# Two-layer transformer block on one core: the opening stages and the store of the rotated halves, arranged anew

## The reference

```python
q = (x @ Wq.T).reshape(B, S, H, hd).transpose(0, 2, 1, 3)   # k and v likewise
q, k = _rope(q), _rope(k)        # [t1*cos - t2*sin, t1*sin + t2*cos], t1, t2: halves of a head
scores = jnp.einsum('bhqd,bhkd->bhqk', q, k) * scale
```

## Time and profile before

| | |
|---|---|
| median of 3 runs | 652.36 us (646.97 to 653.94) |
| the profiled execution | 647.78 us, its span 646.1 us |
| PE busy | 549.5 us (85%) |
| DVE busy | 396.2 us (61%) |
| ACT busy | 309.1 us (48%) |
| POOL busy | 212.8 us (33%) |

### The profile page before, as it was taken

One profiled execution on the slowest core, in us unless ns is written; L12 is line 12 of the kernel. 1 busy time (PEld: TensorE's weight loads), 2 busy tenths in 40 slices (PEclk: granted clock), 3 DMA queues, 4 the chain that ended last, 5 costly groups with the idle time before them and its releaser, 6 DMA issues.

```text
span 646.1 us, 10027 instructions
## 1 busy us (share of the span) xinstructions
PE 549.5 (85%) x3586; PEld 308.5 (48%) x3586; DVE 396.2 (61%) x932; ACT 309.1 (48%) x589; POOL 212.8 (33%) x276
## 2 busy tenths in 40 slices
PE   2877989787879897799878998999999999899873
PEld 1833435434435454444435555545575446643632
DVE  6368887576767555565765576756656765434463
ACT  2223756575455752466435555554435432564221
POOL 4544543242633731650352311414331110220101
PEclk9576999999899898899989999999999999999998
DMA  8461214211343462201561122125404120000000
GB/s 225 107 171 42 77 38 97 68 53 58 136 113 62 98 156 90 100 35 59 107 166 65 57 51 47 41 80 128 89 14 91 27 51 1 19 2 0 1 17 16
DMA packets 28545, 46.15 MB, mean 71 GB/s; under 512 B 5104, under 2 KB 14352, under 8 KB 27920
## 3 DMA queue, kind: packets, MB, share of 16 engines
q1 hardware_dynamic: 28496, 45.52, 27.4%
HBM read 27.22 MB, written 17.83 MB: 70 GB/s over the span
## 4 chain that ended last, share of the span: by engine, by line
PE 57%; DVE 20%; ACT 6%; issue 5%; SPq 5%; DMA 3%; POOL 3%; POOLq 0%; DVEq 0%; ACTq 0%
PE ps L565 11%; PE ps L522 9%; PE ps L628 8%; DVE NM L1124 6%; PE ps L493 5%; PE ps L490 4%; PE ps L495 4%; PE ps L516 2%; DVE terms L1224 2%; PE ps L650 2%; PE ps L748 2%; DVE stats L1108 2%; PE ps L674 2%; PE ps L572 1%; PE ps L611 1%
## 5 line engine op out<-in xcount | busy, mean ns | idle before, releaser
L1124 DVE TENSOR_REDUCE NM<-ps 128x1 f32<-128x512 f32 (+3 forms) x352 | 219.5, 639 | 120.0 <-PE ps L495 113.0
L785 ACT ACTIVATE PG<-ps 128x512 f32<-128x512 f32 x320 | 181.4, 596 | 160.9 <-PE ps L522 93.6
L522 PE MATMUL ps<-QS,K 128*128 128x512 f32 x320 | 118.6, 455 | 0.6 <-DMA QS<-MP 0.6
L495 PE MATMUL ps<-maskb,identb 128*128 128x128 bf16 x512 | 111.1, 235 | 0.0
L565 PE MATMUL ps<-PG,V 128*32 128x512 f32 (+3 forms) x1024 | 98.4, 458 | 6.7 <-POOL PG L1070 5.2
L493 PE MATMUL ps<-K,QS 96*128 96x256 f32 (+3 forms) x256 | 84.8, 375 | 15.4 <-DVE NM L1124 15.1
L490 PE MATMUL ps<-KS,QS 96*128 96x256 bf16 (+3 forms) x256 | 74.7, 327 | 20.5 <-DVE NM L1124 19.3
L495 PEld LDWEIGHTS ps<-maskb,identb 128*128 128x128 bf16 x512 | 52.4, 102 | 38.7 <-issue 31.4
L522 PEld LDWEIGHTS ps<-QS,K 128*128 128x128 f32 x320 | 51.6, 195 | 39.6 <-issue 21.1
L516 PE MATMUL ps<-QS,KS 128*128 128x128 bf16 (+3 forms) x256 | 63.8, 311 | 6.3 <-DMA QS<-scr 4.2
L1029 POOL TENSOR_TENSOR whole<-terms 128x512 f32<-128x512 f32 x28 | 35.4, 1273 | 101.4 <-DVE terms L1224 65.1
(11 more groups left out here) (153 smaller groups left out, 658.6 us busy)
## 6 DMA issues: line engine op xcount, KB each, us to landing
scr<-QC SPq DMA_DIRECT2D x24, 512.0 KB, 3.1
QS<-scr SPq DMA_DIRECT2D x64, 128.0 KB
QS<-scr_q SPq DMA_DIRECT2D x16, 288.0 KB
KS<-scr_k SPq DMA_DIRECT2D x16, 288.0 KB
QS<-scr SPq DMA_DIRECT2D x64, 64.0 KB
scr_k<-room SPq DMA_DIRECT2D x40, 64.0 KB, 2.1
scr_q<-room SPq DMA_DIRECT2D x24, 64.0 KB, 2.1
x<-in_x SPq DMA_DIRECT2D x4, 256.0 KB, 5.8
```

Of the source, the lines that this page charges most:

```text
L495: return pe.matmul(dst[:, P * (k - 1):P * k], identb[:], maskb[:, 0, :], start=False, stop=True)
L522: mm = pe.matmul(bank.rearrange("p (h q) -> p h q", h=HG), keys[:, SEQ[n] % 2, P * j:P * j + P], QS2[:, heads, P * i:P * i + P], start=(ke ...
L785: act.activation(PG[:, n % 2, unit_place(LAYER[n], (u + k) % UNITS), :], ps[:, ST0 + (u + k) % 3, :], ACT.Exp, scale=scale).then_inc(exp_d ...
L1124: dve.tensor_reduce(dst, src, AX.X, ALU.max, negate=True).then_inc(fill_read, 1)
```

## The change

- The scratch of layer 1 becomes one tensor with both halves of a part side by side. `halves` is [part, half, token] in place of `up` and `vp`. The outputs of the projection are ordered anew, so that U holds channels 0 to 3 of q and of k, and V channels 4 to 7. store1 is 5 DMAs of 256 KB from 128 partitions. load1 reads the same 72 rows from the new layout.
- The projection's weights are loaded plain (one DMA of 512-byte pieces, with v's) and put in order by two DVE copies into `wuv_sb`. The rotation table is loaded in 8 DMAs of 16 rows. QKV_LOADS has 9 DMAs.
- The weight product takes four heads at once: weights with 128 rows, `wkvb_sb` with four blocks on a diagonal of zeros, 64 columns: 8 matmuls. DVE clears `wkvb_sb` before all else. The operands come in 12 DMAs of 32 partitions from ACT's queue, at the head of its program, behind a wait for the clear. LOADS keeps 12.
- Of batch 0, DVE makes the V half's join and its two subtractions, and ln1n in place of ACT.
- One semaphore for each half or buffer replaces the shared ones.

```diff
-        QKV_LOADS = ((wqkv_sb[:, 0:2, 0:64], wqkv[:, 0].rearrange("c (a m) -> c a m", a=2)),
-                     (wqkv_sb[:, 0, 64:P], wqkv[:, 2, 64:P]), (wqkv_sb[:, 1, 64:P], wqkv[:, 2, 0:64]),
-                     (wqkv_sb[:, 2], wqkv[:, 4]), (rope1_sb[:], rope1[:]))
-        LOADS = ((wqn_sb, wq_nope[:]), (wo2_sb, wo2[:]), (wkvb_sb, wkvb[:]), (erow_sb, expert_rows[:]),
+        QKV_LOADS = [(wqkv_sb[:], wqkv[:, 0:5:2])]
+        QKV_LOADS += [(rope1_sb[2 * H * d + H * s:2 * H * d + H * s + H], rope1[H * d:H * d + H]) for d in range(D1 // 2) for s in range(2)]
+        LOADS = ((erow_sb, expert_rows[:]),
...
+        BLOCK_LOADS = []
+        for h in range(HG):
+            rows, heads = slice(NOPE * h, NOPE * h + NOPE), slice(G * h, G * h + G)
+            BLOCK_LOADS += [(wqn_sb[rows], wq_nope[:, heads]), (wo2_sb[rows], wo2[:, heads]), (wkvb_sb[rows, :, h, :], wkvb[:, heads])]
...
-                    sp.wait_ge(ready, 2 * (b + 1))
-                    sp.dma_start(scr_q[b, a, 0:64], up[0:64, a, :]).then_inc(stored1, 16)
-                    sp.dma_start(scr_q[b, a, 64:P], vp[0:64, a, :]).then_inc(stored1, 16)
+                    for k in range(2):
+                        sp.wait_ge(ready[k], b + 1)
                     for copy in ((a, 3 + a) if a < 2 else (a,)):
-                        sp.dma_start(scr_k[b, copy, 0:64], vp[64:P, a, :]).then_inc(stored1, 16)
-                        sp.dma_start(scr_k[b, copy, 64:P], up[64:P, a, :]).then_inc(stored1, 16)
+                        sp.dma_start(scr_1[b, copy].rearrange("k p t -> p k t"), halves[:, a]).then_inc(stored1, 16)
...
-                    for h in range(H):
-                        mm = pe.matmul(dst[:, LAT * h:LAT * h + LAT], w[:, h, :], wkvb_sb[:, h, :], start=True, stop=True)
+                    for g in range(G):
+                        mm = pe.matmul(dst[:, 0:H * LAT].rearrange("c (h g r) -> c g h r", h=HG, g=G)[:, g], w[:, g, :],
+                                       wkvb_sb[:, g], start=True, stop=True)
...
+            act.wait_ge(blocks_zero, 1)
+            for dst, src in BLOCK_LOADS:
+                act.dma_start(dst, src).then_inc(loaded, 16)
...
+                dve.wait_ge(loaded_qkv, ALL_QKV)
+                for k in range(2):
+                    dve.tensor_copy(wuv_sb[:, k, :].rearrange("c (d s h) -> c d s h", d=D1 // 2, s=2),
+                                    wqkv_sb[:, 0:2, P // 2 * k:P // 2 * k + P // 2].rearrange("c s (d h) -> c d s h", h=H))                       .then_inc(wuv_ready, 1)
                 dve.wait_ge(consts_ready, STACK_ZEROS)
...
+                if b == 0:
+                    dve.tensor_tensor(whole[:, j % 2, :], terms[:, j % 2, 0, :], terms[:, j % 2, 1, :], ALU.subtract)\
+                       .then_inc(whole_ready[j % 2], 1)
+
+            def parts1(b, _):
+                if b == 0:
+                    j = JOB0["k1", 0, 0] % 2
+                    dve.wait_ge(high1[1], 1)
+                    dve.tensor_tensor(terms[:, j, 0, :], whole[:, j, :], halves[:, 0, 1, :], ALU.subtract).then_inc(rest1[1], 1)
...
+            def ln1n(b, _):
+                if b == 0:
+                    dve.wait_ge(scale_ready, SCALE_OF["ln1n", 0])
+                    for t in range(NT):
+                        last = dve.tensor_scalar(xn[:, t, :], xs[0][:, t, :], rstd[0][:, t:t + 1], nmean[0][:, t:t + 1],
+                                                 ALU.mult, ALU.add)
+                    last.then_inc(xn_ready, 1)
...
+            dve.memset(wkvb_sb.rearrange("p g h r -> p (g h r)"), 0.0).then_inc(blocks_zero, 1)
             dve.memset(KS1[64:P].bitcast(F32), 0.0).then_inc(consts_ready, 1)
```

More of the change, by code:

```diff
@@ L304, in block_program @@
         room1 = sb("room1", [P, 4 * T])
[L305 to L306 removed]
+        halves = room1[:, 0:3 * T].bitcast(BF16).rearrange("p (a k t) -> p a k t", a=3, k=2)
         xT1 = room1[:, 3 * T:4 * T]
@@ L436, in load1 @@
                 heads = slice(HG * g, HG * g + HG)
[L437 to L440, removed]
+                first = 10 * b * P + HG * g
+                rows = [[2 * H * T, 3 * D1], [0, 3], [1, HG * T]]
+                sp.dma_start(QS1[0:72, heads, :], bass.AP(scr_1, first * T, rows)).then_inc(stack1_in[g], 16)
+                rows = [[2 * H * T, 3 * D1], [2 * P * T, 3], [1, HG * T]]
+                sp.dma_start(KS1[0:72, heads, :], bass.AP(scr_1, (first + H) * T, rows)).then_inc(stack1_in[g], 16)
             def store2(stage):
@@ L819, in parts1 @@
             def parts1(b, _):
-                for k, (stage, parts) in enumerate((("q1", up), ("k1", vp))):
+                for k, stage in enumerate(("q1", "k1")):
                     j = JOB0[stage, b, 0]
-                    act.wait_ge(whole_ready, j + 1)
+                    act.wait_ge(*joined(j))
                     if b and k == 0:
                         act.wait_ge(stored1, STORED1 * b)
-                    act.activation(parts[:, 0, :], whole[:, j % 2, :], ACT.Copy).then_inc(high1, 1)
+                    act.activation(halves[:, 0, k, :], whole[:, j % 2, :], ACT.Copy).then_inc(high1[k], 1)
             def parts1b(b, _):
-                for k, (stage, parts) in enumerate((("q1", up), ("k1", vp))):
+                for k, stage in enumerate(("q1", "k1")):
                     j = JOB0[stage, b, 0]
-                    act.wait_ge(rest1, 2 * b + k + 1)
-                    act.activation(parts[:, 1, :], terms[:, j % 2, 0, :], ACT.Copy).then_inc(middle1, 1)
+                    act.wait_ge(rest1[k], b + 1)
+                    act.activation(halves[:, 1, k, :], terms[:, j % 2, 0, :], ACT.Copy).then_inc(middle1[k], 1)
             def v1(b, _):
@@ L1027, in _ @@
                     j = JOB0[stage, b, part]
+                    if stage == "k1" and b == 0:
+                        return
                     pool.wait_ge(terms_ready, j + 1)
                     pool.tensor_tensor(whole[:, j % 2, :], terms[:, j % 2, 0, :], terms[:, j % 2, 1, :], ops[part % 2])\
[L1030 removed]
+                        .then_inc(whole_ready[j % 2], 1)
                 return _
             def parts1(b, _):
[L1034 removed]
+                for k, stage in enumerate(("q1", "k1")):
                     j = JOB0[stage, b, 0] % 2
[L1036 to L1037 removed]
+                    if b == 0 and k == 1:
+                        break
+                    pool.wait_ge(high1[k], b + 1)
+                    pool.tensor_tensor(terms[:, j, 0, :], whole[:, j, :], halves[:, 0, k, :], ALU.subtract).then_inc(rest1[k], 1)
             def parts1b(b, _):
[L1040 removed]
+                for k, stage in enumerate(("q1", "k1")):
                     j = JOB0[stage, b, 0] % 2
[L1042 to L1044 removed]
+                    if b == 0 and k == 1:
+                        break
+                    pool.wait_ge(middle1[k], b + 1)
+                    pool.tensor_tensor(halves[:, 2, k, :], terms[:, j, 0, :], halves[:, 1, k, :], ALU.subtract).then_inc(low1[k], 1)
+                    pool.wait_ge(low1[k], b + 1)
                     pool.sem_inc(job_done[j], 1)
```

52 lines of the change are left out of this document (30 added, 22 removed).

## The result

| | before | after |
|---|---|---|
| median | 653.15 us (4 runs, 646.97 to 655.77) | 643.50 us (4 runs, 640.79 to 645.14) |
| profiled execution | 647.78 us, span 646.1 | 640.79 us, span 638.8 |

The ratio of after to before is 0.9866, 95% interval 0.9821 to 0.9910: 1.3% faster. A second measurement gave 0.9868 (0.9825 to 0.9911), with medians of 653.52 (23 runs of before) and 643.72 (6 runs of after).

A forecast was written before the change was run, and what follows sets the result against it. Two almost equally long queues, PE's weight product and SP's sixteen stores, were taken to bound the first score. Terms -6.5 - 1.6 - 0.6 = -8.7 us gave 639.1 profiled, 643.7 on the median; range 636 to 651.

The forecast's parts named there:

- Opening: Start of the kernel up to the first score: batch 1's projection and first score 6.5 us earlier, score near 32.0.
- the step on the loads: SP's nine opening loads: last issued near 6.1, landed 9.5 to 10.5; cost 0 to 1.4 us through DVE's clear.
- a rival (646.5 with 2 to 3 us lost): Opening loads land late, at 12 to 13, and batch 0 loses 2 to 3 of the 6.5 us: 646.5, chance 0.20.
- DVE and POOL side by side: Batch 0's V half on DVE beside U on POOL: the engines exclude each other, 0.5 us more, V ends at 21.7.
- Norm on DVE: Batch 0's norm: four DVE operations in 0.87 us where ACT's took 1.66, -0.8 us.
- Twelve issues on ACT: Twelve opening loads on ACT's queue: 0.45 us each, done near 8, no cost; up to +1 if issues are dear.
- DVE's first clear: Memset of 128x256 ahead of everything on DVE: +0.22 us on the chain.
- The bytes are the same: Opening loads on a second queue: same bytes and 16 engines, so no bandwidth gain, zero in the sum.
- Weight product: Batch 0's product on PE at L650: 2.3 to 3.4 us instead of 13.36, off the path to batch 1's projection.
- Slower: Rival: without the long weight product PE's clock rises later and the gain is lost: 659, chance 0.10.
- Group 0's load: Load before the first scores: 4.9 us to land, in by 31.3 at the latest, slack 0.7 us.
- Later stalls: PE's waits behind SP's stores at batch 2 (-1.6) and batch 3 (-0.6) vanish.

The follow-up runs named there:

- the table early: Changed kernel with the rotation table loaded in one DMA, rows put in order by the host: first score 32.06 us, total 640.54 us.
- POOL's clear: Changed kernel with the clear of the rows from 96 given to POOL instead of DVE: first score 34.46 us.
- product only: Kernel before with eight block matmuls, their clear and twelve loads on ACT's queue, sixteen stores kept: ratio 1.0000, first score 37.85 us.
- sixteen stores for all: Changed kernel with every batch's store, batch 0's too, cut into 16 DMAs: total 652.22 us, first score 38.33 us.
- statistics first: Changed kernel with one-load table, projection awaiting weights alone, rows from 96 cleared by POOL, batch 1's statistics before V's low part: ratio 0.9820, median 640.21 us.
- the store alone: Kernel before with only the new layout, copies, nine opening loads and five stores a batch: ratio 0.9936, first score 40.81 us.

## Why the prediction came out

The total was forecast as 643.7 and is 643.5; the gain on the medians 8.7 forecast, 9.7 measured, between the two profiled executions 7.0. The mechanism is the forecast one: PE's queue and SP's both shortened, and the first score earlier only with both. That the total agrees to 0.2 us is luck: two terms of the sum were mis-sized, in opposite directions, and the median of before, 652.36 in three runs, is 653.15 with the fourth.

- *Opening, -6.5 forecast, -4.9 measured.* Mis-sized was the step on the loads. The last piece of the table was put at 9.5 to 10.5, no cost up to 10.6. It was issued at 6.08, as forecast, and landed 5.44 us later, at 11.52. And behind the copies stood 0.91 us of issue before the clear, which the forecast had not counted. In the chain of waits of after:

```profile
6.08 5.44 DMA rope_sb<-in_rope
...
11.91 0.91 issue
12.82 1.30 DVE KS L1226
```

  The clear ended at 16.29, not at 13.7 to 14.5. The prediction gave this as a rival (646.5 with 2 to 3 us lost); it came true, with 1.6 us lost. With the table early the first score is at 32.06, where the forecast had 32.0.
- *DVE and POOL side by side.* The two operations lose 0.9 us (1.06 + 1.20 instead of 2 x 0.69), where the forecast allowed 0.5. From the rotation's end to V's low part it is 4.5 us (18.80 to 23.29), where the forecast had 4.6 (17.1 to 21.7): the stage is right, the 1.6 us stand ahead of it. The Trainium skill, SBUF — State Buffer, "Who interferes with whom", says that such a pair, a VectorE operation with two SBUF inputs and a GpSimd one that reads SBUF, excludes each other; the trace agrees in both operations (1.06 and 1.20 us instead of 0.69). The copies beside POOL's clear, 1.86 us instead of 0.36, are another pair and no evidence for that sentence.
- *V half on DVE instead of POOL:* worth 0.8 us at the first score, against the kernel that undoes it.
- *Norm on DVE:* 1.11 us at 8.64, 0.87 forecast. *Twelve issues on ACT:* 0.44 us each, over at 6.87, 8 forecast. *DVE's first clear:* +0.39 us on the statistics (5.60 against 5.21), +0.22 forecast. It runs from 0.91 to 1.18, and the next clear then begins at 2.09, behind 0.91 us of issue.
- *"The bytes are the same", no bandwidth gain.* That misses the order in time: with ACT's loads beside them the eight pieces of the table, which the chain waits for, landed after 4.5 us instead of 2.4.
- *Weight product:* 3.89 us against 2.3 to 3.4; off the path, as forecast. The lower bound came from the V product in 1.16 us, which ran at the high clock (see "Slower"), while in after both products ran at the low one. *Store:* 3.33 us for five, within 2.2 to 4.2, landing after 2.5 us. *Group 0's load:* 4.9 us forecast; where the score waited for it, it took 5.1 us (product only), 5.6 (sixteen stores for all) and 6.9 (statistics first), so the 0.7 us of slack in the forecast were no safe margin, though in after the trace shows no wait for this load.
- *Later stalls, -2.2 forecast.* The price was read from one execution, which happened to stall briefly and to keep its clock. Over four executions with sixteen stores the two places are worth 3.8 (before) to 7.7 us (1.7 to 5.6, and 2.1). This can have made up for the opening on the medians; that the median execution of before stalls long is not shown.
- *Slower, because the clock rises later.* It rises sooner, with the scores. The windows of after have to be read with care:

```profile
19.00:38.50 19.50, 13.96 (x55) 9.23 (x56) 10.70 (x25) 6.49 (x13) 7.04 (x8) 1.00 0.62 175
38.50:46.50 8.00, 5.89 (x29) 2.23 (x28) 7.18 (x12) 1.67 (x3) 7.61 (x6) 0.65 0.62 199
46.50:60.20 13.70, 11.47 (x61) 6.18 (x62) 10.77 (x22) 4.99 (x9) 4.08 (x3) 0.58 0.00 1
```

  The 1.00 of the first line, where the earlier trace rows has 0.51, is not the clock that PE had. The trace of this execution has no entry for the clock before 34.05 us, where it records a rise, and a stretch without an entry is printed as 1.00. The matmuls tell the rest: the V product took 2.08 us instead of 1.16, and the scores on both sides of the rise are

```profile
33.60 0.61 PE L496 MATMUL ps<-KS,QS 96*128 96x512 bf16 x1
36.78 0.38 PE L496 MATMUL ps<-KS,QS 96*128 96x512 bf16 x1
```

  So PE ran at 1.2 GHz up to 34.05, as in before, where the rise is at 39.74. Then 17.1 us at the low clock follow from 40.9, in before 13.7 from 46.6, and between two issues of maxima there (54.8 and 63.5 in before, 49.9 and 59.3 in after) the lead falls from 4.9 to 4.2 us. In a second execution of the change the entries show 0.50 from 20 to 32, with the first score at 33.63: both ran that stretch at half clock, so the two don't tell what the clock is worth there.

How far single executions go apart limits all this. From the issue of maxima behind batch 3's store (222.45 in before) to the last but one store of the output (617.16) nothing differs between the kernels but where batch 3's loads read; before took 394.7 us there, after 397.4, and the thirteen executions other than before 396.4 to 401.7, mean 398.9. The profiled execution of before was thus 4 us luckier than the others in a part that the change hardly touches, and it kept its clock at batch 2. It stands 5.4 us under the median of before, that of after 2.7 under its own: the difference is the 2.7 us between 7.0 and 9.7.

## What to carry to other kernels

When two queues of nearly equal length end at one wait, price the parts together: here the product alone brought 0.65 us at the first score, the store alone lost 2.3 (late constants ahead of a product that still held PE), both brought 4.9. A stall of PE in a dense stretch is priced with what the clock does behind it, and from more than one execution. Loads moved to a second queue start sooner and make the first queue's later: put on it what nobody waits for, and give the urgent load few pieces, issued early (14.78 instead of 16.32 for the rotation here). Starting the second queue's loads only once the urgent ones have landed would be another way; no run tried it. And before a printed clock of 1.00 is believed, the duration of a matmul of known shape is compared.

## What was not expected of the hardware

- A clear on DVE behind another operation has 0.91 us of "issue" before it, at L1226 and at the clear that begins at 2.09. Before had 0.89 at L1202 too, off the path. No run tells what the engine does in it.
- A small piece of the table (64 KB) lands after 2.4 us with one queue at work and 4.5 with two, the last after 5.4; in one piece of 512 KB the table took 4.4 us with one queue and 6.6 with two.
- The eight matmuls of batch 0's V product took 1.16 us in five executions, 2.07 or 2.08 in eight and 1.74 in one, though the views print a clock of 1.00 over most of them. In the five the entries have the clock at 1.00 there and falling to 0.50 behind the product, in the one it falls within it, and in the eight there is no entry at all before 31 us, where a rise is the first. PE had 2.4 GHz for a few microseconds in six executions and not in the eight; why, no run shows. It was off the path.
